# Mixing stage of a convolution-and-experts block: the right operand's columns sorted, the result stored in rows three times as long

## The reference, cut to what matters

```python
left = (xn @ Wl + bl) * jax.nn.sigmoid(xn @ Wlg + blg)
right = (xn @ Wr + br) * jax.nn.sigmoid(xn @ Wrg + brg)
out_gate = jax.nn.sigmoid(xn @ Wog + bog)
out = jnp.einsum('bkjd,bkid->bijd', left, right) / n      # n = 384
out = layer_norm(out, on_a, on_b) * out_gate
x = x + out @ Wo + bo
```

## Time and profile before

| | us |
|---|---|
| median of 3 runs | 2889.62 |
| lowest and highest | 2883.52, 2896.89 |
| the profiled execution | 2896.19 |
| its span (first to last instruction) | 2894.4 |

### The profile page before, as it was taken

One profiled execution on the slowest core, in us unless ns is written; L12 is line 12 of the kernel. 1 busy time (PEld: TensorE's weight loads), 2 busy tenths in 40 slices (PEclk: granted clock), 3 DMA queues, 4 the chain that ended last, 5 costly groups with the idle time before them and its releaser, 6 DMA issues.

```text
span 2894.4 us, 65116 instructions
## 1 busy us (share of the span) xinstructions
PE 2609.9 (90%) x15070; PEld 2141.5 (74%) x15070; DVE 2415.4 (83%) x4683; ACT 2253.1 (78%) x4278; POOL 1828.9 (63%) x1911
## 2 busy tenths in 40 slices
PE   6999999999999998999999999489899898898935
PEld 5888888888888887988898898366666666666623
DVE  6777777777777776999999999889999888989862
ACT  5888888888888887788888888478888888888840
POOL 8888888888888886000000000099999999999941
PEclk9999999999999999999999999799999999999977
DMA  5777777777777776899999999599999999999946
GB/s 185 264 271 272 268 265 273 270 264 272 272 267 266 274 270 252 315 334 332 339 324 339 333 338 332 185 354 364 366 365 368 362 356 359 364 359 359 363 137 213
DMA packets 281418, 873.06 MB, mean 302 GB/s; under 512 B 29479, under 2 KB 81858, under 8 KB 281378
## 3 DMA queue, kind: packets, MB, share of 16 engines
q1 hardware_dynamic: 272322, 855.31, 80.4%
q10 hardware_dynamic: 8704, 16.78, 2.0%
q0 software_dynamic: 352, 0.53, 0.2%
HBM read 492.97 MB, written 379.52 MB: 301 GB/s over the span
## 4 chain that ended last, share of the span: by engine, by line
PE 43%; DMA 21%; DVE 9%; issue 9%; POOL 8%; ACT 5%; SPq 3%; DVEq 1%; POOLq 0%; ACTq 0%
PE banks L1285 34%; DMA arena<-left_d 12%; DMA work<-gate_d 7%; PE banks L1274 4%; POOL arena L689 3%; POOL arena L695 2%; DVE bn L1102 2%; ACT arena L825 2%; ACT work L895 2%; PE banks L1320 1%; DVE arena L1093 1%; PE banks L1371 1%; POOL rs L712 1%; DMA work<-in_x_dram 1%; DVE arena L1082 1%
## 5 line engine op out<-in xcount | busy, mean ns | idle before, releaser
L1285 PE MATMUL banks<-x_parts,w_parts 128*128 128x512 f32 x4320 | 1068.0, 399 | 0.0
L1285 PEld LDWEIGHTS banks<-x_parts,w_parts 128*128 128x128 f32 x4320 | 791.7, 189 | 161.7
L1320 PE MATMUL banks<-left_parts,right_parts 128*128 128x384 f32 x3456 | 629.1, 340 | 60.3 <-ACT arena L826 49.5
L1320 PEld LDWEIGHTS banks<-left_parts,right_parts 128*128 128x128 f32 x3456 | 603.7, 190 | 85.8 <-issue 81.7
L973 DVE SCALAR_TENSOR_TENSOR arena<-banks,cols,arena 128x512 f32<-128x512 f32 x576 | 407.0, 748 | 246.9 <-ACT arena L791 245.1
L684 POOL COPY rcol<-late 128x8 f32 (+1 forms) x144 | 28.4, 197 | 715.1 <-ACT late L841 715.1
L895 ACT ACTIVATE work<-arena,rs 128x128 f32<-128x128 f32 x1152 | 352.5, 389 | 128.1 <-POOL rs L712 128.1
L1353 PE MATMUL banks<-wo_sb,arena 128*128 128x128 f32 x2304 | 396.2, 301 | 9.1 <-DVE arena L1093 8.6
L689 POOL TENSOR_TENSOR arena<-arena,work 128x512 f32<-128x512 f32 x288 | 359.7, 1270 | 61.9 <-DVE arena L1082 61.2
L1353 PEld LDWEIGHTS banks<-wo_sb,arena 128*128 128x128 f32 x2304 | 359.8, 192 | 50.1 <-issue 21.1
L651 POOL TENSOR_TENSOR x_parts<-xn,x_parts 128x512 fp32r<-128x512 f32 x288 | 372.0, 1292 | 6.6 <-ACT x_parts L779 6.6
(11 more groups left out here) (177 smaller groups left out, 4165.9 us busy)
## 6 DMA issues: line engine op xcount, KB each, us to landing
arena<-in_x_dram SPq DMA_DIRECT2D x144, 512.0 KB, 3.4
left_d<-arena SPq DMA_DIRECT2D x144, 512.0 KB, 2.6
right_d<-arena SPq DMA_DIRECT2D x144, 512.0 KB, 3.4
gate_d<-arena SPq DMA_DIRECT2D x144, 512.0 KB, 4.2
arena<-right_d SPq DMA_DIRECT2D x128, 576.0 KB, 5.7
arena<-left_d SPq DMA_DIRECT2D x128, 576.0 KB, 6.7
mixed_d<-arena SPq DMA_DIRECT2D x128, 576.0 KB, 4.4
work<-mixed_d SPq DMA_DIRECT2D x144, 512.0 KB, 4.8
```

The costliest lines, as they stand in the source:

```text
L1285: last = nc.tensor.matmul(ps[2 + k][:, :], w_parts[:, wq, k], x_parts[:, xq, b, c], start=((wq, xq) == TERMS[0]), stop=((wq, xq) == TERMS[ ...
L1320: last = nc.tensor.matmul(ps[NT * b + t][:, 0:GRID], lr_parts[RIGHT][:, rq, b, k, t * P:(t + 1) * P], lr_parts[LEFT][:, lq, b, k], start=( ...
```

## The change

The stored row order becomes 3r+t instead of t*128+r: the views `mixed_w` and `stat_w` are now `(p t j)`, so that each partition's three runs join to one, of 4608 bytes for `mixed_d` and 2304 bytes for each plane of `stat_d`. For this the column at place t*128+r of the right operand has to be column 3r+t. The right cast (ACT) and the right subtraction (DVE) do that as they go: both read `rch` with a stride of three floats (12 bytes) and write without a gap; the low half is formed from the already sorted high half. Matmuls, evacuation and sums are as before, on permuted rows. The nine small copies of reciprocal deviations write every ninth float in place of every third. No instruction, wait or DMA is added or taken away.

```diff
-        mixed_w = mixed_d.rearrange("c (t p j) -> c p t j", t=NT, p=P)
-        stat_w = stat_d.rearrange("q (t p j) -> q p t j", t=NT, p=P)
+        mixed_w = mixed_d.rearrange("c (p t j) -> c p t j", t=NT, p=P)
+        stat_w = stat_d.rearrange("q (p t j) -> q p t j", t=NT, p=P)
+
+        def sorted_rows(plane):
+            return plane.rearrange("p k (r t) -> p k t r", t=NT)
+
+        def row_tiles(plane):
+            return plane.rearrange("p k (t r) -> p k t r", t=NT)
...
-                nc.scalar.copy(lr_parts[RIGHT][:, HI, b], rch[:, b]).then_inc(s_hi2, 1)
+                nc.scalar.copy(row_tiles(lr_parts[RIGHT][:, HI, b]), sorted_rows(rch[:, b])).then_inc(s_hi2, 1)
...
-                    nc.scalar.copy(rstd_grid[:, t * P:(t + 1) * P, c], ps[n % 2][:, 0:P]).then_inc(s_rtc, 1)
+                    nc.scalar.copy(rstd_grid[:, t::NT, c], ps[n % 2][:, 0:P]).then_inc(s_rtc, 1)
...
-                for n, (side, whole) in enumerate(((RIGHT, rch), (LEFT, lch))):
-                    dve.wait_ge(s_hi2, mark(2, 2 * i + b, n + 1))
-                    parts = lr_parts[side]
-                    nc.vector.tensor_tensor(parts[:, LO, b], whole[:, b], parts[:, HI, b], ALU.subtract).then_inc(s_lo2, 1)
+                dve.wait_ge(s_hi2, mark(2, 2 * i + b, 1))
+                parts = lr_parts[RIGHT]
+                nc.vector.tensor_tensor(row_tiles(parts[:, LO, b]), sorted_rows(rch[:, b]), row_tiles(parts[:, HI, b]),
+                                        ALU.subtract).then_inc(s_lo2, 1)
+                dve.wait_ge(s_hi2, mark(2, 2 * i + b, 2))
+                parts = lr_parts[LEFT]
+                nc.vector.tensor_tensor(parts[:, LO, b], lch[:, b], parts[:, HI, b], ALU.subtract).then_inc(s_lo2, 1)
```

## The result

The changed kernel takes 2939.7 us (median of 6 runs, 2937.6 to 2948.5), the kernel before, beside it, 2892.4 us. The ratio is 1.0172, with a 95% interval of 1.0150 to 1.0194: it is slower by 47 us. The prediction had 2927, with 2876 to 2956.

What follows compares the result with a forecast made beforehand. DVE bounds stage 2 in most channels, a load-cast-subtraction ring in some. DVE's 5.08 + 0.46 = 5.54, plus 0.03 waiting, gives 5.57 against 5.27 us per channel: +38, with hand-over +37; 2889.6 + 37 = 2927 us, range 2876 to 2956.

Steps and rivals of the forecast that it cites:

- The floor: DVE's four instructions per stage 2 channel: 5.08 us, rising by 0.46 for the strided right subtraction to 5.54.
- The memory's pace and not the engine's: Strided access on DVE and ACT: nearly one time per scattered element, some 1.8 and 1.91 ns, looks set by memory.
- The cast: ACT's strided right cast in stage 2: +0.6 us, between 0 and +0.88.
- The waits: DVE's waiting above its floor in stage 2: 0.19 us per channel before, 0.03 left after the change.
- the ring: Stage 2's right load, casts, subtractions, store and next load: 10.70 us per two channels, then about 10.7 + 0.2 - 0.1 + 0.46.
- two floors: DVE's instruction time for two channels, compared with one ring: 10.16 us before, 11.08 forecast.
- The store: Stage 2's result store in longer runs: 0.11 us less per ring, worth 0.06 per channel, 7 us in all.
- The hand-over: After stage 2: last `stat_d` stores -0.4 us, the nine copies +0.3; the total went from +38 to +37 us.
- Rivals 1 and 2: Stage 2: DVE reads 12-byte steps free, ACT pays: 2880 us, chance 0.32; neither pays: 2873 us, chance 0.12.
- rival 3: Right subtraction: DVE pays the whole element again, +1.2 us, period 6.28, 3017 us in all; chance 0.10.
- rival 4: Result store: runs don't join and stay 1536-byte packets, its 7 us gain gone; chance spread over rivals 1 and 2.
- The turning point: Right subtraction on DVE: the change's sign turns at an extra cost of +0.19 us.

Runs made afterwards that it cites:

- e8: A kernel of its own running single 1152-element instructions alone: DVE's subtraction took 1.359 us contiguous, 1.69 at a step of 3 floats, 2.199 at 4.
- e4: The changed kernel with both strided reads kept, but stores in 1536- and 768-byte runs as before: 5.61 us per channel, 1.0122 of the kernel before.
- e1: The changed kernel with cast and subtraction reading without a stride, only the long runs kept: 5.38 us per channel, 1.0030 of the kernel before.

## Why the prediction was right, and where it wasn't

**The floor.** Right. The strided subtraction sets most of the new time, and it pays at the price of scattered access; forecast +0.46 us, measured +0.39. The row L841 gave 1.62 ns per element for 12 bytes; e8 has 1.33. L841 itself shows where the difference went: with a step of 36 bytes the same copy takes 392 ns in place of 334, and 58/128 = 0.45 ns is just 1.78 less 1.33. So the rest of the 334 ns, 164, is fixed, and not the 126 that was taken from larger copies. L1225's 1.8 ns per scattered write agrees with the 1.78 of wide reads (e8 has no wide write on DVE). L953, the row against, was rightly set aside: alternating runs are free on DVE (1.376 us). That this is because each piece is used whole isn't shown, as ACT pays for the same order (1.411 us against 1.151). "The memory's pace and not the engine's" holds for the subtraction and ACT's copies, but a plain copy on DVE paid half.

**The cast.** Forecast +0.6, measured +0.62.

**The waits.** This step failed: I left 0.03 us of remaining wait, it was 0.22. The prediction added +0.2 to the ring for the cast and +0.46 for the subtraction, gave the load 0.1 and a further gain without a number "because the DMA engines are then under less pressure", and found the ring "at or below two floors". The turn came to 11.48, against 10.94 for two floors. Landing to cast grew by 0.13 us, cast to right subtraction by 0.73 and right to left subtraction by 0.36; left subtraction to next load shrank by only 0.24. That makes 1.0 where the prediction had 0.66. (It let SP take up 0.3 us, though its own times, 1526.20 against 1526.71, differ by 0.51.) The load gained only 0.09. A gain was there: in e4, with both strides and short packets, the load lands 0.28 sooner than before. The long packets, which the prediction counted as a gain, took 0.19 of it back. Even in e4 0.14 us of waiting is left. So of the 0.19 us that were missed, about 0.11 lie in the ring's own sum and 0.08 in the store.

That is 0.19 x 127 = 24 us too little, against 0.07 x 127 = 9 us that the subtraction was too dear: stage 2 grew by 53 us and not by 38. The medians differ by 47, against 37 forecast. That the forecast came so near is partly luck, for the subtraction's error offset a third of that in the waits.

**The store.** Wrong in sign. Forecast 0.06 us less per channel, measured 0.07 to 0.11 more (e1, e4). The rate in isolation, 373 against 402 GB/s, is true of a store that runs alone and says nothing of its neighbours.

**The hand-over.** From the last stores of `stat_d` to the first load, which waits for them, 3.75 us instead of 4.25, about as forecast; from the last store of `mixed_d` to the first load of `stat_d` 35.3 instead of 35.5. The nine copies went from 334 to 392 ns each, hidden. The prediction's own terms, -0.4 and +0.3, make -0.1 and not the -1 between its +38 and +37; the 35.3 and 35.5 bear out the -0.1.

**The rivals.** Rivals 1 and 2 (DVE reads for free, neither pays) and rival 3 (the whole element again) fall with the 1.74 us, and rival 4 with the packets that joined. The turning point wasn't +0.19 us for the subtraction: e1 is slower with no stride at all, so with this store no price of the subtraction would have made the change faster.

## What to carry to other kernels

Ask what one scattered element costs before moving a permutation to a compute engine: here 1.78 ns per 16 bytes touched in DVE's subtraction and about as much in ACT's copy, half of that in DVE's plain copy, and free at 8 bytes in the subtraction; at 12 bytes the instruction took a quarter longer on DVE and half as long again on ACT. Count a ring of load, cast and free buffer as a second floor beside the busiest engine's, with the new durations in it; it grew a little more than the floor here, and moving one wait gave back 0.17 of the 0.42 us per channel that were lost. And a longer run isn't worth its isolated rate: measure it among the transfers that it shares the engines with.

## What the runs showed that I had not expected

- Beside a store in 4608-byte packets the right loads land 0.17 to 0.26 us later than beside the same store in 1536-byte packets, and in e1 at a DMA share of 0.91 in place of 0.95.
- Loads issued ahead of the store, which then goes a step later, cost 1.7%. The 4608-byte packets' mean time rose from 210 to 251 ns, and the evacuation waited for the late store.
- A TensorE weight load with a step of 12 bytes takes 252 ns in place of 188, and hides.
- DVE's plain copy reads with a step of 8 floats in 1.198 us, DVE's subtraction in 2.222.
- ACT pays for two alternating runs (1.41 against 1.15 us), DVE doesn't (1.376 against 1.359).
